# A mixture-of-experts stage: one region of rows per expert for all four batches, 39 blocks in an order made on the chip, results written back into their rows, first scatters spread over attention

## The chip, the core and the metric

The kernel runs on one core of one Trainium2 chip. The metric is the device time of one execution in microseconds (us).

## The reference, cut to what matters

The input is four batches of 1024 tokens of 128 features. Two transformer layers follow each other; the second is the one in question:

```python
x1 = layernorm(x + attention(x))              # 16 heads of 8, not causal
topk_p, topk_i = top_k(softmax(x1 @ Wg), 2)   # 8 experts, 2 per token
comb = one_hot(topk_i) * topk_p / sum(topk_p)
h = gelu(x1 @ W1[e] + b1[e])                  # 128 -> 512, for each expert e
y = h @ W2[e] + b2[e]                         # 512 -> 128
out = x + layernorm(x1 + sum_e comb[e] * y[e])
```

## The kernel before

Everything is written out by hand for each engine: TensorE, VectorE (DVE), ScalarE (ACT), GpSimd (POOL) and SyncE (SP), which issues nearly all plain DMAs in the order of its program. Semaphores join them.

**Attention.** The second layer's attention runs over 16 groups of four heads (0 to 15), four groups per batch. A group has 32 units; in each unit TensorE makes two score blocks (L613), ScalarE their exponentials (L709), TensorE the value products (L628), and for the next group a chunk of scores (L585) of which VectorE takes row maxima (L664). GpSimd stores each half of a group's head outputs (L750), prepares the next group's values and the maxima's bfloat16 parts (L758 on). Its `fronts` are called at point 0 (before the first store), 1 (before the maxima's parts) and 2 (after the second store).

**Fronts.** When a batch's four groups are done, its rows go through the output projection (L1467), the norm (roots on GpSimd, L1276), a transpose (L855), the gate's logits (L1480) and the choice of two experts. Batches 0 and 1 do so in groups 7 and 11, batch 2 in group 15, batch 3 beside the first blocks. `ranks` (L1484) counts on TensorE how many tokens chose each expert before this one; `sort` (L1771) turns that into a slot number for each token and choice.

**Scatter, blocks, gather.** `scatter` (L1299) writes each tile of 128 rows to its slots with an indirect DMA on GpSimd, two per tile. At most two are on the way: `ON_WAY`, `landed`. There are two sections: batches 0 and 1 (one sort in group 12), and batches 2 and 3 (two sorts). A section is worked off in 23 blocks of 256 rows, 2 x 16 x 128 / 256 = 16 full ones and up to 7 for the rests of 8 experts. `list_blocks` (L1795) works out on VectorE which expert a block belongs to. For block m, `load_expert` (L1080) fetches 578 KB of weights (4 buffers) and `load_rows` (L1089) 128 KB of rows (6 buffers); TensorE turns the rows (L1503), multiplies up (L1512), and multiplies down one block later (L1522). ScalarE makes the gelu (L2090), VectorE adds the bias (L1837), and `store_y` (L1104) writes the results to a second DRAM tensor. The experts and rows of the first blocks are loaded in group 14 (L1115 to L1130).

`gather` (L1315) picks each token's two results, eight indirect DMAs per half batch, two on the way in the first section and four in the second; VectorE combines them (L1840), GpSimd takes a root (L1334), ScalarE normalises (L2093), VectorE finishes (L1865), SP stores. The first section's gathers wait for its 23 blocks and run beside the second section; the second section's wait for all 46. The positions of all this in the block loop are written by hand (L904 to L909).

Numbers of a register are read by SP with `value_load`, for the expert of every block and, in the second section, for its rows.

## Time and profile before

| | us |
|---|---|
| median of three runs | 1621.58 |
| lowest, highest | 1619.73, 1623.44 |
| the profiled execution's own time | 1623.35 |
| its span in the trace | 1621.6 |

| engine | busy us | share |
|---|---|---|
| TensorE matmul | 1400.8 | 86% |
| VectorE | 1223.4 | 75% |
| ScalarE | 1141.0 | 70% |
| GpSimd | 481.0 | 30% |

The span is cut at attention's end (1363 us) and the last down (1559 us). Times in the rows count from the span's start. PE is TensorE, DVE VectorE, ACT ScalarE, POOL GpSimd, SPq SyncE's DMA queue. What stands in brackets behind a row is the engine's idle time before it and what ended that time.

### The profile page before, as it was taken

The page shows a single profiled execution, that of the slowest core. Times are in us where ns is not written, and L with a number is a line of the kernel's source. Part 1 is how long each engine was busy: PE and PEld are TensorE (multiplying, and loading weights), DVE is VectorE, ACT ScalarE, POOL GpSimd, SP SyncE. Part 2 cuts the span into 40 slices and gives each one's busy share as a digit, 9 for nine tenths or more (in the row PEclk, how much of TensorE's full clock was granted, in tenths as well). Part 3 has the DMA queues.
Part 4 walks back from the last instruction along what each step waited for, and adds up shares of the span by engine and source line. Part 5 has one row for each costly group of instructions (what it writes and reads, how often), then busy time and mean ns, then how long its engine had stood idle before and what let it go on. Part 6 is the DMA issues. An engine that isn't in the chain of part 4 may idle for free.

```text
span 1621.6 us, 36086 instructions
## 1 busy us (share of the span) xinstructions
PE 1400.8 (86%) x13425; PEld 604.9 (37%) x13425; DVE 1223.4 (75%) x1846; ACT 1141.0 (70%) x2357; POOL 481.0 (30%) x786
## 2 busy tenths in 40 slices
PE   5679999999998888479999999999988999899940
PEld 2323333333333555112222223222322235888830
DVE  6788888888881665799999998999898852432444
ACT  7628888888888455129999997999777786334421
POOL 5413333433334564200000003000314322332455
PEclk9959999999999999659999999999999899999975
DMA  4622212112112363401333331113101411778942
GB/s 137 196 79 74 69 41 72 55 56 74 44 51 75 100 178 95 152 5 48 118 126 125 106 89 43 42 49 90 36 28 62 133 38 59 217 232 242 275 134 57
DMA packets 130255, 158.26 MB, mean 98 GB/s; under 512 B 17312, under 2 KB 103328, under 8 KB 129824
## 3 DMA queue, kind: packets, MB, share of 16 engines
q1 hardware_dynamic: 120864, 130.77, 25.8%
q0 software_dynamic: 9216, 25.18, 4.5%
q8 instruction: 107, 1.75, 0.5%
q14 instruction: 68, 0.56, 0.1%
HBM read 90.90 MB, written 68.96 MB: 99 GB/s over the span
## 4 chain that ended last, share of the span: by engine, by line
PE 43%; DVE 10%; issue 6%; DMA 4%; ACT 2%; SPq 1%; POOL 1%; another core or an unknown queue 0%; POOLq 0%; DVEq 0%; ACTq 0%
PE bank L628 16%; PE banks L613 10%; DVE row_max L664 6%; PE banks L585 6%; PE banks L1522 4%; PE banks L1512 4%; DMA qk_parts<-parts 2%; ACT o_sums L724 1%; DMA parts<-sorted_in 1%; PE banks L1503 1%; PE banks L337 0%; PE banks L1467 0%; PE banks L1480 0%; DMA expert<-expert_rows 0%; DMA heads_out<-o_sums 0%
## 5 line engine op out<-in xcount | busy, mean ns | idle before, releaser
L664 DVE TENSOR_REDUCE row_max<-banks 128x2 f32<-128x1024 f32 (+3 forms) x896 | 936.4, 1104 | 77.5 <-PE banks L585 41.4
L709 ACT ACTIVATE probs<-banks 128x512 f32<-128x512 f32 (+3 forms) x1792 | 874.9, 552 | 134.8 <-PE banks L613 109.6
L628 PE MATMUL bank<-probs,v_ones 128*32 128x256 f32 (+2 forms) x6656 | 527.3, 389 | 11.7 <-ACT o_sums L724 10.5
L585 PE MATMUL banks<-k_work,q_work 48*128 48x512 bf16 (+3 forms) x1792 | 364.3, 379 | 62.9 <-DVE row_max L664 48.2
L613 PE MATMUL banks<-q_work,k_work 51*128 51x512 bf16 (+3 forms) x1792 | 383.8, 370 | 18.1 <-ACT probs L709 12.6
L613 PEld LDWEIGHTS banks<-q_work,k_work 51*128 51x128 bf16 x1792 | 105.6, 93 | 394.5 <-ACT probs L709 340.6
L628 PEld LDWEIGHTS bank<-probs,v_ones 128*32 128x32 f32 x6656 | 134.1, 108 | 262.5 <-ACT probs L709 169.5
L750 POOL DMA_DIRECT2D heads_out<-o_sums x64 | 36.7, 573 | 498.0 <-ACT o_sums L724 498.0
L2090 ACT ACTIVATE rope<-banks,expert 128x256 f32<-128x256 f32 x184 | 72.2, 475 | 111.6 <-PE banks L1512 96.9
L770 POOL TENSOR_SCALAR_AFFINE_SELECT probs<-probs 128x256 f32<-128x256 f32 x256 | 103.9, 409 | 124.8 <-ACT probs L709 124.1
L585 PEld LDWEIGHTS banks<-k_work,q_work 48*128 48x128 bf16 x1792 | 90.6, 96 | 120.0 <-DVE row_max L664 90.9
L1512 PE MATMUL banks<-rope,expert 128*128 128x256 f32 x368 | 89.6, 387 | 7.2 <-issue 6.6
L1522 PE MATMUL banks<-expert,rope 128*128 128x128 f32 x736 | 91.1, 278 | 0.8 <-DVE k_work L1837 0.8
L1522 PEld LDWEIGHTS banks<-expert,rope 128*128 128x128 f32 x736 | 87.1, 194 | 1.2 <-ACT rope L2090 0.8
L337 PE MATMUL banks<-hT,w_qk 128*128 128x512 f32 x128 | 67.2, 656 | 21.8 <-ACT hT L400 11.8
L1312 POOL DMA_INDIRECT sorted_in<-v_all,slots x64 | 62.0, 968 | 59.1 <-DMA sorted_in<-v_all,slots 45.3
L1512 PEld LDWEIGHTS banks<-rope,expert 128*128 128x128 f32 x368 | 67.7, 194 | 15.7 <-issue 8.1
L591 PE MATMUL banks<-later_keys,half_ident 64*128 64x128 bf16 (+1 forms) x1024 | 72.3, 210 | 0.0
L1829 DVE COPY rope<-banks 128x256 f32<-128x256 f32 x46 | 19.4, 422 | 64.4 <-PE banks L1503 53.9
L758 POOL CAST max_parts<-top_max 128x32 bf16<-128x32 f32 x32 | 6.7, 209 | 202.3 <-DVE top_max L672 202.3
L591 PEld LDWEIGHTS banks<-later_keys,half_ident 64*128 64x128 bf16 x1024 | 55.8, 99 | 23.4 <-issue 2.7
L383 POOL TENSOR_TENSOR parts<-probs,parts 128x1024 bf16<-128x1024 f32 x16 | 34.1, 2129 | 74.5 <-ACT parts L418 74.5
(195 smaller groups left out, 1035.0 us busy)
## 6 DMA issues: line engine op xcount, KB each, us to landing
expert<-expert_rows SPq DMA_DIRECT2D x46, 578.0 KB
qk_parts<-parts SPq DMA_DIRECT2D x64, 256.0 KB, 3.5
heads_out<-o_sums POOLq DMA_DIRECT2D x64, 256.0 KB, 4.2
sorted_in<-front SPq DMA_DIRECT2D x21, 512.0 KB, 6.1
q_work<-qk_parts SPq DMA_DIRECT2D x64, 128.0 KB
k_work<-qk_parts SPq DMA_DIRECT2D x64, 128.0 KB
parts<-sorted_in SPq DMA_DIRECT2D x46, 128.0 KB
q_work<-qk_parts SPq DMA_DIRECT2D x64, 64.0 KB
```

The costliest lines, as they stand in the source:

```text
L337: pe.matmul(bank[QK_BANK + u % QK_BANKS], w_qk[a][:, i, :], hT[:, :], start=True, stop=True).then_inc(s["qk"], 1)
L585: last = pe.matmul(to[:, par, 0:width], q[r:r + M0, pair, qt * P:(qt + 1) * P], k[r:r + M0, pair, kh * G:kh * G + width], start=True, stop ...
L591: last = pe.matmul(to[:, par, width - P + c0:width], half_ident[r:r + HALF, half, :], later_keys[r:r + HALF, half, c0:P], start=False, sto ...
L613: pe.matmul(to[par][:, 0:G - c0], k[r:r + M1, pair, kt * P:(kt + 1) * P], q[r:r + M1, pair, qh * G + c0:(qh + 1) * G], start=True, stop=Tr ...
L628: last = pe.matmul(bank[7][32 * j:32 * j + 32, c0 + c1:c0 + c1 + w], v_ones[i % QB][:, kt, j, :], prob_slots[:, (e + j) % RING, c1:c1 + w] ...
L664: dve.tensor_reduce(row_max[:, :, pair, qt, kh], self.buf_of("chunk", g, c)[:, :, 0:width], AX.X, ALU.max).then_inc(s["chunk_max"], 1)
L709: act.activation(prob_slots[:, e % RING, 0:width], self.ring_bank("exp", e)[:, 0:width], ACT.Exp, scale=SCALE).then_inc(s["exps"], 1)
L770: pool.affine_select(here, here, [[0, 2], [1, P]], ALU.is_ge, 0.0, base=0, channel_multiplier=-1).then_inc(s["blanked"], 1)
L1312: pool.indirect_dma_start(xs_d[section], bass.IndirectOffsetOnAxis(slots[:, section, i, tile:tile + 1], 0), x1_rows[:, ST * section + tile ...
L1512: last = pe.matmul(hidden(m, f), expert[:, m % W_BUFS, f * P:(f + 1) * P], xsT[:, m % 2, :], start=True, stop=True)
L1522: last = pe.matmul(bank[Y_BANK][:, side * P:(side + 1) * P], h_block[:, m % 2, f, side * P:(side + 1) * P], expert[:, m % W_BUFS, FF + f * ...
L2090: act.activation(h_block[:, m % 2, f, :], hidden(m, f), ACT.Gelu, bias=expert[:, m % W_BUFS, 2 * FF + f:2 * FF + f + 1]).then_inc(end["gel ...
```

## The change

There is one region of 4096 rows (16 blocks) for each expert in a single DRAM tensor, so that all four batches are worked off in 2 x 32 x 128 / 256 + 7 = 39 blocks. Each of the 128 possible blocks of the regions is a candidate, one per partition. `list_grades` gives each a grade: blocks filled by batches 0 and 1 first, then those filled with batch 2, then the others. TensorE spreads the keys to all partitions, VectorE counts the lower ones, and the result is the list of block rows and experts. FULL is (9, 17, 25): so many blocks are surely full after batch 1, 2 and 3. The list is made in two parts, for blocks 0 to 16 after batch 2's sort and for 17 to 38 at blocks 11 to 13 of the loop. Rows of block 9 wait for batch 2's scatters, those of block 17 for batch 3's. DONE is (25, 31, 39): after 25 stored blocks batches 0 and 1 are complete, after 31 batch 2, after 39 batch 3. `store_y` writes to the rows that the block was read from; the gathers use the scatters' own slots, with four on the way (GATHERED). The scatters of the first section are issued one tile at a time, each behind a wait for ScalarE's exponentials of a given unit, in groups 12 to 15. The loads of the first experts and rows go from group 14 to behind the sums of batch 3. The tensor to be zeroed has 32 runs of 512 KB in place of 23. `place` and the old list go.

```diff
-BLOCKS = TOPK * ST // SIDES + E - 1
...
+BLOCKS = TOPK * B * TILES // SIDES + E - 1
...
+SEEN = (ST, ST + TILES, ST + 2 * TILES)
+FULL = tuple(-(-(TOPK * n * P - E * (BR - 1)) // BR) for n in SEEN)
+HELD = tuple((TOPK * n * P + E * (BR - 1)) // BR for n in SEEN)
+LISTED = (0, FULL[1], BLOCKS)
+LISTS = len(LISTED) - 1
+READY = (0, FULL[0], FULL[1])
+DONE = (max(FULL[1] + E, HELD[0]), HELD[1], BLOCKS)
...
-        SCATTER_AT = ((0, 1, 0, 3), (0, 2, 3, 10), (1, 1, 10, 12), (1, 2, 12, ST))
+        SCATTER_AT = ((0, 1, 20),) + tuple((g, at, u) for g in (1, 2) for at, u in ((0, 3), (0, 7), (0, 11), (0, 15), (1, 20)))
+        SCATTER_AT += ((3, 0, 11), (3, 0, 14), (3, 0, 17), (3, 1, 20), (3, 1, 23))
...
-        ROWS_FROM, ROWS_LATE = BLOCKS - 3, (2, 2, 1)
-        LOAD_AT, COMBINE_AT, MOMENTS_LATE = (4, 8, 12, 16, 18, 21), (8, 13, 17, 22), (9, 14, 18)
-        NORMAL_AT, FINISH_AT, OUT_AT = (13, 18, 22), (14, 19), (15, 20)
-        ROWS_FROM, ROWS_LATE = BLOCKS - 3, (2, 2, 1)
+        LIST_AT = (11, 12, 13)
+        AHEAD_OF = {FULL[0]: 2, FULL[1]: 2}
+        LOAD_AT, COMBINE_AT, MOMENTS_LATE = (20, 21, 22, 23), (31, 34, 37), (32, 35, 38)
+        NORMAL_AT, FINISH_AT, OUT_AT = (34, 37), (35, 38), (37,)
         FOLD_UNIT, PRODUCT_FIRST, APPLY_FIRST, TURN_FIRST, INPUT_FIRST = 2, 8, 14, 17, 19
...
             def load_expert(m):
-                section, j = divmod(m, BLOCKS)
-                sp.wait_ge(end["blocks"], section + 1)
+                sp.wait_ge(end["blocks"], 1 if m < LISTED[1] else 2)
                 if m >= W_BUFS:
                     sp.wait_ge(end["y"], m - W_BUFS + 1)
-                which = sp.value_load(block_expert[0:1, section, j:j + 1], min_val=0, max_val=E - 1)
+                which = sp.value_load(block_expert[0:1, m:m + 1], min_val=0, max_val=E - 1)
                 sp.dma_start(expert[:, m % W_BUFS, :], expert_d[bass.ds(which, 1), :, :].rearrange("o p r -> (o p) r")
                              ).then_inc(w_here[m % W_BUFS], 16)
 
             def load_rows(m):
-                section, j = divmod(m, BLOCKS)
-                if j == 0:
-                    wait_lanes(sp, scatter_number(section * (STAGES - 1), TOPK * (TILES if section else ST) - 1))
+                if m in READY:
+                    stage = READY.index(m)
+                    wait_lanes(sp, scatter_number(stage, TOPK * (ST if stage == 0 else TILES) - 1))
+                sp.wait_ge(end["blocks"], 1 if m < LISTED[1] else 2)
                 if m >= X_BUFS:
-                if section:
-                    sp.wait_ge(end["blocks"], section + 1)
-                    which = sp.value_load(block_row[0:1, j:j + 1], min_val=0, max_val=REGION - 1)
-                    src = rows[bass.ds(which, 1), :, :, :].rearrange("o p k d -> (o p) k d")
-                else:
-                    src = rows[j, :, :, :]
+                which = sp.value_load(block_row[0:1, m:m + 1], min_val=0, max_val=REGION - 1)
+                src = xs_blocks[bass.ds(which, 1), :, :, :].rearrange("o p k d -> (o p) k d")
                 sp.dma_start(xs_in[:, m % X_BUFS, :, :], src).then_inc(xs_here[m % X_BUFS], 16)
 
             def store_y(m):
-                section, j = divmod(m, BLOCKS)
                 sp.wait_ge(end["y"], m + 1)
-                to = ys_d[section].rearrange("(n k p) d -> n p k d", k=SIDES, p=P)[j, :, :, :]
-                sp.dma_start(to, y_of(m)).then_inc(y_out[section], 16)
+                which = sp.value_load(block_row[0:1, m:m + 1], min_val=0, max_val=REGION - 1)
+                to = xs_blocks[bass.ds(which, 1), :, :, :].rearrange("o p k d -> (o p) k d")
+                sp.dma_start(to, y_of(m)).then_inc(y_out[done_of(m)], 16)
 
...
-                if i == NG - 2:
-                    sp.wait_ge(mid["x_out"], 16 * GROUPS)
-                    sp.wait_ge(rows_made, 16 * len(made))
-                    for m in range(W_BUFS):
-                        load_expert(m)
 
...
             attend[2].load_sums(sp, B - 1)
+            sp.wait_ge(mid["x_out"], 16 * GROUPS)
+            sp.wait_ge(rows_made, 16 * len(made))
+            for m in range(2):
+                load_expert(m)
+                load_rows(m)
             attend[2].store_reciprocals(sp, B - 1)
-            load_expert(W_BUFS)
+            for m in range(2, W_BUFS):
+                load_expert(m)
+                load_rows(m)
             for k in range(HALVES):
                 load_front(B - 1, k)
...
+            loaded_rows = W_BUFS
+            for m in range(BLOCKS):
+                if 0 < m and m + W_BUFS - 1 < BLOCKS:
+                    load_expert(m + W_BUFS - 1)
+                while loaded_rows < min(m + X_BUFS, BLOCKS):
+                    late_from = max((x for x in AHEAD_OF if x <= loaded_rows), default=None)
+                    if late_from is not None and m < late_from - AHEAD_OF[late_from] + (loaded_rows - late_from) // 2:
+                        break
+                    load_rows(loaded_rows)
+                    loaded_rows += 1
...
             def gather(n):
                 section, h = divmod(n, SETS)
-                if h == 0:
-                    pool.wait_ge(y_out[section], 16 * BLOCKS)
-                    if section:
-                        pool.wait_ge(end["placed"], 1)
+                if n % HALVES == 0 and n != HALVES:
+                    pool.wait_ge(y_out[max(n // HALVES - 1, 0)], 16 * (DONE[0], DONE[1] - DONE[0], DONE[2] - DONE[1])[max(n // HALVES - 1, 0)])
                 if section:
                     pool.wait_ge(end["sum"], GT * (n - SETS + 1))
...
-                for group, at, a, b in SCATTER_AT:
+                for tile, (group, at, u) in enumerate(SCATTER_AT):
                     if (i, point) == (SORT_GROUP + group, at):
-                        scatter(0, a, b)
+                        pool.wait_ge(attend[2].s["exps"], i * attend[2].ne + 2 * u)
+                        scatter(0, tile, tile + 1)
...
+            def list_keys(n, to):
+                pe.wait_ge(end["keyed"], 2 * n + 1)
+                pe.matmul(to[:, 0:P], ones_b[:, :], graded[:, :], start=True, stop=True).then_inc(end["listed"], 1)
+
+            def list_rows(n, to):
+                a, b = LISTED[n:n + 2]
+                pe.wait_ge(end["keyed"], 2 * n + 2)
+                pe.matmul(to[:, P:P + b - a], ids_b[:, :], found[:, 0:b - a], start=True, stop=True)
+                pe.matmul(to[:, 2 * P:2 * P + b - a], experts_b[:, :], found[:, 0:b - a], start=True,
+                          stop=True).then_inc(end["listed"], 1)
+
...
             pe.wait_ge(attend[2].s["exps"], NG * attend[2].ne)
+            list_keys(0, bank[LIST_BANK[0]])
+            list_rows(0, bank[LIST_BANK[0]])
             turn_rows(0)
...
+            def count(stage):
+                a, b = STAGE_TILES[stage]
+                n = b - a
+                dve.wait_ge(end["ranks"], stage + 1)
+                base = seen[:, stage - 1:stage, :] if stage else region[:, :, :]
+                total = rank_bank(stage)[:, n * E:(n + 1) * E].rearrange("p (o e) -> p o e", o=1)
+                link(dve.tensor_tensor(seen[:, stage:stage + 1, :], total, base, ALU.add))
...
-                    list_blocks(0)
-                    link(dve.tensor_scalar(first_slot[:, :, :], start_of[:, :, :], float(SIDES * P), None, ALU.mult))
-                link(dve.tensor_tensor(slot_te[:, a:b, :], within, base[:, :, :].broadcast_to([P, n, E]), ALU.add))
+                link(dve.tensor_tensor(slot_te[:, a:b, :], within, base.broadcast_to([P, n, E]), ALU.add))
                 for i in range(TOPK):
                     last = dve.tensor_tensor(slot_pick[:, i, a:b, :], chosen[:, i, a:b, :], slot_te[:, a:b, :], ALU.mult)
...
-            def list_blocks(section):
...
-            def place():
...
+            def list_grades(n):
+                stages = n + 2
+                link(dve.tensor_tensor(seen_own[:, 0:stages, :], seen[:, 0:stages, :],
+                                       own_expert[:, :, :].broadcast_to([P, stages, E]), ALU.mult))
+                link(dve.tensor_reduce(filled[:, 0:stages], seen_own[:, 0:stages, :], AX.X, ALU.add))
+                link(dve.tensor_scalar(filled[:, 0:stages], filled[:, 0:stages], own_start[:, 0:1], None, ALU.subtract))
+                dve.tensor_scalar(whole[:, 0:stages], filled[:, 0:stages], float(BR), None, ALU.is_ge)
+                link(dve.tensor_scalar(begun[:, 0:stages], filled[:, 0:stages], 1.0, None, ALU.is_ge))
+                nearer, among = (whole[:, 0:1], whole[:, 1:2]) if n == 0 else (begun[:, 1:2], begun[:, 2:3])
+                link(dve.tensor_tensor(grade[:, :], begun[:, 0:1], nearer, ALU.add))
+                link(dve.scalar_tensor_tensor(grade[:, :], grade[:, :], 1.0, among, ALU.add, ALU.mult))
+                if n:
+                    link(dve.scalar_tensor_tensor(grade[:, :], taken[:, :], 0.0, grade[:, :], ALU.is_equal, ALU.mult))
+                    link(dve.tensor_tensor(grade[:, :], grade[:, :], taken[:, :], ALU.subtract))
+                link(dve.tensor_scalar(grade[:, :], grade[:, :], -1.0, 3.0, ALU.mult, ALU.add))
+                dve.tensor_tensor(own_key[:, :], own_share[:, :], grade[:, :], ALU.add)
+                dve.tensor_scalar(graded[:, :], ident_b[:, :], grade[:, 0:1], None, ALU.mult).then_inc(end["keyed"], 1)
+
+            def list_places(n, to):
+                a, b = LISTED[n:n + 2]
+                dve.wait_ge(end["listed"], 2 * n + 1)
+                link(dve.tensor_tensor(keys[:, :], to[:, 0:P], row_share[:, :], ALU.add))
+                link(dve.tensor_scalar(lower[:, :], keys[:, :], own_key[:, 0:1], None, ALU.is_lt))
+                link(dve.tensor_reduce(place[:, :], lower[:, :], AX.X, ALU.add))
+                if n == 0:
+                    dve.tensor_scalar(taken[:, :], place[:, :], float(b), None, ALU.is_lt)
+                dve.tensor_scalar(found[:, 0:b - a], row_ids[:, 0:b - a], place[:, 0:1], None, ALU.is_equal).then_inc(end["keyed"], 1)
+
+            def list_blocks(n, to):
+                a, b = LISTED[n:n + 2]
+                dve.wait_ge(end["listed"], 2 * n + 2)
+                dve.tensor_copy(block_row[:, a:b], to[:, P:P + b - a])
+                dve.tensor_copy(block_expert[:, a:b], to[:, 2 * P:2 * P + b - a]).then_inc(end["blocks"], 1)
 
```

## Rows read from the trace of the kernel before

**Rows 1.** The page's 40 slices of 40.5 us, TensorE's busy tenths.

```profile
PE   5679999999998888479999999999988999899940
```

**Rows 2.** Busy time per stretch (us), granted clock, DMA share, GB/s.

```profile
1470.00:1480.00 10.00, 10.00 (x70) 9.33 (x70) 2.12 (x5) 3.96 (x11) 1.96 (x2) 1.00 0.80 240
```

**Rows 3.** TensorE's timeline (start, us, engine, line), ups of two blocks.

```profile
1471.06 1.89 PE L1512 MATMUL banks<-rope,expert 128*128 128x256 f32 x8
...
1474.79 1.89 PE L1512 MATMUL banks<-rope,expert 128*128 128x256 f32 x8
```

**Rows 4.** GpSimd's timeline, gathers, first and last of each bunch.

```profile
1477.64 1.00 POOL L1331 DMA_INDIRECT probs<-sorted_out,slots  x1 [23.18 <-DMA sorted_out<-q_work]
...
1512.11 0.95 POOL L1331 DMA_INDIRECT probs<-sorted_out,slots  x1 [1.97 <-DMA probs<-sorted_out,slots]
...
1563.33 1.02 POOL L1331 DMA_INDIRECT probs<-sorted_out,places  x1 [0.58 <-issue]
...
1604.58 0.94 POOL L1331 DMA_INDIRECT probs<-sorted_out,places  x1 [0.30 <-issue]
```

**Rows 5.** GpSimd's timeline, stores of head outputs, two per group of heads.

```profile
1107.34 0.56 POOL L750 DMA_DIRECT2D heads_out<-o_sums  x1 [11.35 <-ACT o_sums L724]
...
1125.73 0.54 POOL L750 DMA_DIRECT2D heads_out<-o_sums  x1 [17.42 <-ACT o_sums L724]
...
1144.58 0.56 POOL L750 DMA_DIRECT2D heads_out<-o_sums  x1 [11.39 <-ACT o_sums L724]
...
1217.05 0.61 POOL L750 DMA_DIRECT2D heads_out<-o_sums  x1 [19.91 <-ACT o_sums L724]
...
1238.31 0.63 POOL L750 DMA_DIRECT2D heads_out<-o_sums  x1 [10.78 <-ACT o_sums L724]
...
1266.54 0.59 POOL L750 DMA_DIRECT2D heads_out<-o_sums  x1 [4.77 <-ACT o_sums L724]
...
1287.12 0.61 POOL L750 DMA_DIRECT2D heads_out<-o_sums  x1 [11.35 <-ACT o_sums L724]
...
1307.88 0.59 POOL L750 DMA_DIRECT2D heads_out<-o_sums  x1 [3.40 <-ACT o_sums L724]
```

**Rows 6.** VectorE's timeline, first sort: first step and the slots' step.

```profile
1199.54 0.16 DVE L1780 COPY total_of<-banks 128x8 f32<-128x8 f32 x1
...
1202.06 0.29 DVE L1783 TENSOR_TENSOR slot_te<-banks,first_slot 128x128 f32<-128x128 f32 x1
```

**Rows 7.** TensorE's timeline within group 13.

```profile
1256.35 0.59 PE L613 MATMUL banks<-q_work,k_work 51*128 51x512 bf16 x1 [2.15 <-issue]
```

**Rows 8.** TensorE's timeline, ups of blocks 0 and 5.

```profile
1363.90 1.96 PE L1512 MATMUL banks<-rope,expert 128*128 128x256 f32 x8 [0.61 <-DVE rope L1829]
...
1387.63 2.83 PE L1512 MATMUL banks<-rope,expert 128*128 128x256 f32 x8
```

**Rows 9.** SyncE's DMA issues: the sums, then block 24's expert, rows, store.

```profile
1367.70 0.60 SPq L508 DMA_DIRECT2D sums_in<-heads_out  x1
...
1472.67 0.35 SPq L1086 DMA_DIRECT2D expert<-expert_rows  x1
1473.85 0.38 SPq L1102 DMA_DIRECT2D parts<-sorted_in  x1
1474.27 0.47 SPq L1108 DMA_DIRECT2D sorted_out<-q_work  x1
```

**Rows 10.** GpSimd's timeline: last store, a root, scatters of batches 2 and 3.

```profile
1363.88 0.54 POOL L750 DMA_DIRECT2D heads_out<-o_sums  x1 [16.62 <-ACT o_sums L724]
...
1398.94 1.01 POOL L1276 TENSOR_TENSOR rstd<-ve,minus_half 128x4 f32<-128x4 f32 x1 [1.85 <-DVE minus_mean L1678]
...
1406.54 0.96 POOL L1312 DMA_INDIRECT sorted_in<-v_all,slots  x1 [0.30 <-issue]
...
1419.37 1.03 POOL L1312 DMA_INDIRECT sorted_in<-v_all,slots  x1 [1.29 <-DVE slots L1793]
...
1453.51 0.96 POOL L1312 DMA_INDIRECT sorted_in<-v_all,slots  x1 [1.61 <-DMA sorted_in<-v_all,slots]
```

344 lines of the change are left out of this document (156 added, 188 removed).

## The prediction

> **What bounds the kernel now.** The page's slices come first [rows 1]: TensorE is busy in eight or nine tenths of nearly every slice up to the last two, where it stands still. So there are three stages to read: attention (to 1363 us), the expert blocks (to 1559 us) and a tail without TensorE (to 1621.6 us).
>
> The stretches of ten microseconds show the block stage more finely [rows 2]: 10.00 of 10 us of TensorE at full clock (1.00, the 2.4 GHz level), DMA share 0.80 before any gather runs. The TensorE timeline gives the price of a block [rows 3]: up to up, 1474.79 - 1471.06 = 3.73 us. Blocks set the pace there, and DMA has little room left.
>
> In the tail the chain is GpSimd's gathers: eight per half batch, 32 of them from 1563.33 to 1604.58, one after the other, then 16.1 us from the end of the last (1605.5) to the span's end [rows 4].
>
> In attention the group of four heads has a steady beat: between two stores of the head outputs 18.39 and 18.85 us, 37.2 us per group [rows 5]. The groups in which the first two batches' rows are scattered are longer.
>
> **Attention, what goes.** (a) The first sort loses its block list: VectorE from the copy at 1199.54 to the sort's own first step at 1202.06 is 2.5 us [rows 6], in a stretch where VectorE's maxima pace the group. Added there is one 8-column addition of 0.2 us. Gain 2.3 us. (b) The scatters. Excess of the half groups over the steady halves [rows 5]: group 12 second half 21.26 - 18.85 = 2.4, group 13 first half 28.23 - 18.39 = 9.8, second half 20.58 - 18.85 = 1.7, group 14 first half 20.76 - 18.39 = 2.4; 16.3 us together, worst where the timeline has 14 scatters between two stores (GpSimd then still waits 4.77 us for ScalarE, so the store is not late by itself). There TensorE idles 2.15 us with nothing to wait for [rows 7]: a freeze behind the bunch. The change issues two scatters at a time, four units (about 4.7 us) apart. Bounds: it saves nothing and adds 3 us (ten scatters now lie in group 15), or it saves all 16. I take 11, two thirds, because the bunches of four to eight cost 2 us and the bunch of fourteen 9.8. The other new waits of GpSimd hold up its stores and maxima parts: those have their input at units 18 and 23, the waits end at 17 and 20 (23 once), so only a microsecond of slack is used: nothing. The 32 fills instead of 23 (16.8 MB instead of 12) run in groups 1 to 4 beside TensorE's work; if that cover were gone, nine more at the 240 GB/s of the block stage [rows 2] would cost 2.2 us each, 20 us. The iotas and the candidates' nine small VectorE steps lie in group 0 and 15, where those engines wait anyway. Attention: -13.3 us.
>
> **The start of the blocks.** Before, four experts and five row blocks are loaded in group 14 and the first up starts at 1363.90. After, the block list needs batch 2, so SP may load experts only behind the sums. VectorE's grades are done in attention's last units; TensorE's two small steps and VectorE's four end near 1365.4. SP however is busy till 1367.70 + 0.6 with the sums. A value read costs SP 0.8 us: from the end of the expert issue at 1473.02 to the row issue at 1473.85 [rows 9]. First expert issued 1369.1, its rows 1370.3; landing estimated at 3.9 us from the last store of 256 KB, issued 1363.88 and awaited till 1367.70 [rows 9, 10]. First up near 1374, ten microseconds late. But before, blocks 0 to 4 took 23.7 us for five times 3.73, because a row load stood behind the sums and the heads [rows 8]; after, those loads come before they are due, and the up of block 5 starts near 1393.5 instead of 1387.63: +5.9 us (bounds +3 and +9).
>
> **Two new waits of SP.** Block 9's rows are only fetched once all 16 scatters of batch 2 have landed. The last four stand behind the two roots of batch 3 (VectorE's moments of blocks 5 and 6): root at 1398.94, fourth issue at 1406.54 [rows 10], so last landing near 1410, with the shift 1416; SP reads and issues, 2.5 us for the rows: 1419. They are due after the up of block 8, 1409.2 with the shift. Stall 10 us plus 1 for the clock (bounds 4 and 14). Queued behind SP's wait are one store and one expert load, both early enough. Before, this had 14 blocks of room.
>
> Block 17's rows need all of batch 3. Its slots come 6.5 us after the up of block 10, 1436 by now. The 16 scatters took 1419.37 to 1453.51 [rows 10], 2.28 us each with two on the way. Block 17's rows are due only at 1454.5, when nine are issued; then SP blocks, its loads dry up, and the remaining seven go at 2.3 falling to 1.3 us. Last landing 1468, rows there 1471.5: stall 17 us, up of block 17 at 1474.7 with slow matmuls. Bounds 8 and 22. The spread grades and keys replace a long list on VectorE there; with TensorE stalled twice anyway I count no gain, and the new keys' matmuls, each shorter than a row's transposes, cost nothing beside it.
>
> **End of the blocks.** Up of block 25: 1474.7 + 8 x 3.73 + 1.0 = 1505.6. Up of block 38: 13 x 3.73 later, 1554.1; the last down ends near 1560.5, against 1559.1 before. So the seven blocks that go (7 x 3.73 = 26.1 us) are spent on the start and the two stalls.
>
> **The gathers.** Before, 32 start at 1477.64 beside the blocks and 32 more at 1563.33. After, all 64 form one chain from the 25th block's store. Its down lies between the ups of blocks 25 and 26, so its result is there at 1509.5; SP then has three value reads per block (expert, rows, store: 3 x 0.8 + 1.2 = 3.6 us against the block's 3.73, no room to catch up), 3.2 us, plus 2 us of backlog from the two rows per block after the stall and the four loads of x; from store to first gather 3.4 us (1474.27 to 1477.64) [rows 4, 9]. First gather 1518.1. Two roots (2 us each) and the rest of 39 us pass while experts still load, at c us per gather: 35/c gathers. The others take 1.25 us, with three roots between them. G = 39 + (64 - 35/c) x 1.25 + 6 = 125 - 44/c. The row has c = 2.3 with two on the way (16 from 1477.64 to 1512.11) and the issue itself allows 1.25 (32 and a root in 41.25 us) [rows 4]; four on the way is new. I take c = 1.5, G = 96 (bounds 90 and 106), nearer to the issue because the share of 0.80 leaves some room.
> The page DMA: Bandwidth & Descriptors of the Trainium skill, section on queues, rings and completion order, says that each DMA engine takes turns between the queues it has work for, packet by packet. By that rule GpSimd's queue would get its turn however full SP's is; it is weighed below as a rival, and no row here has four gathers beside the loads.
>
> **The sum.** 1518.1 + 96 + 16.1 - 13.3 = 1616.9 against the span of 1621.6: -4.8 with rounding. The profiled execution's own time was 1623.35, the median of the three runs 1621.58; I put the difference on the median: 1616.8 us. What a measurement of this kernel can tell from no change is about 0.2%, 3.2 us.
>
> **Rivals.**
> *Gathers held back (slower).* Four on the way only lengthen each landing, since the loads fill most of the DMA engines. c stays 2.3, G 106: 1626.6. For it: the share of 0.80 before they begin [rows 2]. Against: gathers are 64 KB each. It ends slower from c = 2.1 up. Chance 0.15.
> *Gathers keep the issue's pace.* Landings of 4.6 us (two times 2.3) with four on the way would hide under four issues of 1.25: c = 1.25, G 90, 1611. Chance 0.10. The Trainium skill's turn-taking between queues, above, would make this the case.
> *The pacing saves nothing.* The freezes belong to each scatter, not to the bunch: +11, 1627.8. Against: 9.8 us in one half only. Chance 0.12.
> *The waits are short.* With fewer row loads the scatters land faster, stalls of 4 and 8 us: -15, near 1602. For it: rows 9 and on are not fetched meanwhile, 128 of 850 KB per block. Against: two on the way, as before [rows 10]. Chance 0.16.
> *SP becomes the bound.* A fourth part more per value read gives 4.2 us per block: from block 17 to 25 +4, 1621, no change. Chance 0.09.
> *The change does not pace or order anything in time* (GpSimd comes late to each named unit; the list is free): as before apart from the tail, no change. Chance 0.04.
> Forecast as summed: 0.34, its own range 1609 to 1625: 0.24 of it below 1618.3, 0.07 within, 0.03 above 1624.8.
>
> **Numbers.** Faster by over 0.2%: 0.16 + 0.10 + 0.24 = 0.50. Within: 0.09 + 0.04 + 0.07 = 0.20. Slower: 0.15 + 0.12 + 0.03 = 0.30. The range reaches from the short waits to the held gathers together with part of the lost pacing: 1601 to 1635.
>
> **What would show it.** The half groups 12 to 14 near 19 to 20 us each, no idle of 2 us with nothing waited for. First up 10 us after attention's end. TensorE idle 10 us before the rows of block 9 and 17 us before block 17, with the granted clock lower behind each. 39 ups, the last near 1541 in the new span. First gather near 1505, with c between 1.25 and 1.8 while experts load, then 1.25; the gathers without a pause from set to set. I am wrong if the stall at block 17 is under 8 us, if the start costs over 15 us, or if the tail after the last down is not within 10 us of the 62.5 of before: that would mean the gather chain was not what ends last.

## The result, and the profile after

| | before | after |
|---|---|---|
| median of 20 runs each, us | 1619.83 | 1611.22 |
| lowest to highest, us | 1611.61 to 1626.31 | 1606.11 to 1618.04 |
| the profiled execution's own time, us | 1623.35 | 1607.74 |
| its span, us | 1621.6 | 1605.8 |

The ratio is 0.9956, its 95% interval 0.9942 to 0.9970: a gain of 0.44%, some 7 us. The two profiled executions are 15.8 us apart, twice as much, because single executions of one kernel lie up to 15 us apart. So the profiles serve to find stages, and the medians to say what a stage is worth.

GpSimd's timeline of the kernel after, stores of the head outputs around groups 12 to 14 (start, us, engine, line, operation; in brackets the idle time before and what ended it):

```profile
1213.61 0.61 POOL L761 DMA_DIRECT2D heads_out<-o_sums  x1 [16.94 <-ACT o_sums L735]
...
1232.45 0.63 POOL L761 DMA_DIRECT2D heads_out<-o_sums  x1 [11.39 <-ACT o_sums L735]
...
1250.85 0.58 POOL L761 DMA_DIRECT2D heads_out<-o_sums  x1 [2.56 <-ACT o_sums L735]
...
1270.46 0.61 POOL L761 DMA_DIRECT2D heads_out<-o_sums  x1 [11.35 <-ACT o_sums L735]
...
1288.85 0.58 POOL L761 DMA_DIRECT2D heads_out<-o_sums  x1 [2.57 <-ACT o_sums L735]
```

They answer to [rows 5]. Group 12's second half takes 18.8 us instead of 21.3, group 13's halves 18.4 and 19.6 instead of 28.2 and 20.6, group 14's first 18.4 instead of 20.8. From the store ahead of group 12 to the last store it is 152.2 us instead of 172.8.

TensorE's timeline of the kernel after: the first rows and ups, then blocks 9, 17 and 25, the last up and the last down:

```profile
1351.93 0.69 PE L1509 MATMUL banks<-ident,parts 128*128 128x128 f32 x2 [8.32 <-DMA parts<-sorted_rows]
1353.22 3.75 PE L1518 MATMUL banks<-rope,expert 128*128 128x256 f32 x8 [0.61 <-DVE rope L1858]
...
1375.45 1.89 PE L1518 MATMUL banks<-rope,expert 128*128 128x256 f32 x8
...
1398.54 0.69 PE L1509 MATMUL banks<-ident,parts 128*128 128x128 f32 x2 [8.21 <-DMA parts<-sorted_rows]
1399.02 3.62 PE L1528 MATMUL banks<-expert,rope 128*128 128x128 f32 x16
...
1448.24 0.69 PE L1509 MATMUL banks<-ident,parts 128*128 128x128 f32 x2 [14.40 <-DMA parts<-sorted_rows]
...
1452.14 2.78 PE L1518 MATMUL banks<-rope,expert 128*128 128x256 f32 x8
...
1484.16 1.99 PE L1518 MATMUL banks<-rope,expert 128*128 128x256 f32 x8 [0.40 <-DMA expert<-expert_rows]
...
1534.16 1.89 PE L1518 MATMUL banks<-rope,expert 128*128 128x256 f32 x8
...
1539.09 2.02 PE L1528 MATMUL banks<-expert,rope 128*128 128x128 f32 x16 [1.25 <-DVE k_work L1865]
```

Three long waits for rows are new: 8.32, 8.21 and 14.40 us (before, the two that there were took 3.62 us, at block 5, and 1.41), each followed by matmuls at half speed (the 16 of a down in 3.62 us instead of 1.95). The 39 blocks need as long from attention's end (1341.83) to the last down's end (1541.1) as the 46 did: 199.3 us, before 196.

GpSimd's gathers in the kernel after, the 1st, 16th, 32nd, 33rd and 64th:

```profile
1496.86 0.99 POOL L1333 DMA_INDIRECT probs<-sorted_rows,slots  x1 [53.04 <-DMA sorted_rows<-v_ones]
...
1516.65 0.95 POOL L1333 DMA_INDIRECT probs<-sorted_rows,slots  x1 [0.30 <-issue]
...
1541.91 0.94 POOL L1333 DMA_INDIRECT probs<-sorted_rows,slots  x1 [0.30 <-issue]
...
1544.74 1.01 POOL L1333 DMA_INDIRECT probs<-sorted_rows,slots  x1 [0.54 <-issue]
...
1588.62 0.95 POOL L1333 DMA_INDIRECT probs<-sorted_rows,slots  x1 [0.30 <-issue]
```

They answer to [rows 4] and form one chain: 92.7 us from the first to the end of the last (1589.57), then 16.2 us to the span's end. While experts still load a gather comes every 1.32 us (15 steps in 19.79 us), before every 2.3 us.

The page's slices of the kernel after, busy tenths in 40.1 us each, answering to [rows 1], and one stretch beside the blocks (the columns of [rows 2], to which it answers):

```profile
PE   5679999999998888469999999999999997779930
...
DVE  6788888888892465699999999999999952231345
...
POOL 5413333334333565300000002100222333240575
```

```profile
1500.00:1510.00 10.00, 10.00 (x70) 9.23 (x69) 2.12 (x5) 3.50 (x10) 6.99 (x8) 1.00 0.91 290
```

TensorE has nothing in the last slice and little in the one before, where VectorE and GpSimd are busy with what follows the gathers. Beside the gathers TensorE is still full at the upper clock level (1.00, 2.4 GHz), with the DMA engines at 0.91 instead of 0.80.

### The profile page after: what moved, and what is told of

It is laid out like the page before. It is cut to its first block, busy times and chain, and to the rows that moved or that the text cites. A ratio compares the mean times of both kernels' runs of the same rounds, so it can differ in the third digit from the quotient of the medians.

```text
span 1605.8 us, 35919 instructions
## 1 busy us (share of the span) xinstructions
PE 1368.5 (85%) x13249; PEld 585.1 (36%) x13249; DVE 1215.3 (76%) x1842; ACT 1130.6 (70%) x2329; POOL 481.9 (30%) x789
## 4 chain that ended last, share of the span: by engine, by line
PE 34%; DVE 10%; DMA 7%; issue 6%; POOL 5%; SPq 3%; ACT 2%; POOLq 0%; ACTq 0%; DVEq 0%
PE bank L639 15%; PE banks L624 9%; DVE row_max L675 7%; PE banks L596 5%; POOL probs L1333 3%; DMA sorted_rows<-v_all,slots 2%; DMA qk_parts<-parts 2%; PE banks L1528 1%; DMA probs<-sorted_rows,slots 1%; PE banks L1518 1%; ACT o_sums L735 1%; DMA parts<-sorted_rows 1%; DMA sums_in<-heads_out 1%; SPq L1133 1%; PE banks L348 1%
## 5 line engine op out<-in xcount | busy, mean ns | idle before, releaser
L596 PE MATMUL banks<-k_work,q_work 48*128 48x512 bf16 (+3 forms) x1792 | 359.5, 377 | 61.7 <-DVE row_max L675 49.0
L624 PE MATMUL banks<-q_work,k_work 51*128 51x512 bf16 (+3 forms) x1792 | 376.9, 368 | 10.9 <-ACT probs L720 9.9
L2127 ACT ACTIVATE rope<-banks,expert 128x256 f32<-128x256 f32 x156 | 61.2, 475 | 115.4 <-PE banks L1518 115.4
L1333 POOL DMA_INDIRECT probs<-sorted_rows,slots x64 | 62.8, 982 | 76.1 <-DMA sorted_rows<-v_ones 53.0
L1518 PE MATMUL banks<-rope,expert 128*128 128x256 f32 x312 | 79.2, 399 | 2.9 <-DMA expert<-expert_rows 1.7
L1317 POOL DMA_INDIRECT sorted_rows<-v_all,slots x64 | 62.5, 977 | 62.6 <-DMA sorted_rows<-v_all,slots 30.1
L1528 PE MATMUL banks<-expert,rope 128*128 128x128 f32 x624 | 79.5, 283 | 1.3 <-DVE k_work L1865 1.3
L1858 DVE COPY rope<-banks 128x256 f32<-128x256 f32 x39 | 16.5, 423 | 82.0 <-PE banks L1509 82.0
L1528 PEld LDWEIGHTS banks<-expert,rope 128*128 128x128 f32 x624 | 76.2, 199 | 1.5 <-issue 1.4
L1518 PEld LDWEIGHTS banks<-rope,expert 128*128 128x128 f32 x312 | 59.1, 200 | 11.5 <-DMA expert<-expert_rows 2.4
```

What stands on the lines that cost most here:

```text
L596: last = pe.matmul(to[:, par, 0:width], q[r:r + M0, pair, qt * P:(qt + 1) * P], k[r:r + M0, pair, kh * G:kh * G + width], start=True, stop ...
L624: pe.matmul(to[par][:, 0:G - c0], k[r:r + M1, pair, kt * P:(kt + 1) * P], q[r:r + M1, pair, qh * G + c0:(qh + 1) * G], start=True, stop=Tr ...
L1317: pool.indirect_dma_start(xs_d, bass.IndirectOffsetOnAxis(slots[:, section, i, tile:tile + 1], 0), x1_rows[:, ST * section + tile, :], Non ...
L1333: pool.indirect_dma_start(y_picked[:, h, i, g, :], None, xs_d, bass.IndirectOffsetOnAxis(slots[:, section, i, tile:tile + 1], 0)).then_inc ...
L1518: last = pe.matmul(hidden(m, f), expert[:, m % W_BUFS, f * P:(f + 1) * P], xsT[:, m % 2, :], start=True, stop=True)
L1528: last = pe.matmul(bank[Y_BANK][:, side * P:(side + 1) * P], h_block[:, m % 2, f, side * P:(side + 1) * P], expert[:, m % W_BUFS, FF + f * ...
```

## The experiments

Each median is of 7 to 12 runs beside 14 to 31 runs of the kernel before on the same chip. There were four chips, A to D.

| run | chip | median us | before us | ratio, interval |
|---|---|---|---|---|
| e0, after unchanged | A | 1610.99 | 1620.62 | 0.9958 [0.9936, 0.9981] |
| e1, after, scatters bunched | A | 1618.98 | 1620.62 | 0.9994 [0.9974, 1.0014] |
| e2, before, scatters paced | A | 1609.48 | 1620.62 | 0.9928 [0.9901, 0.9956] |
| e3, after, tiles first | B | 1633.03 | 1631.07 | 1.0014 [0.9991, 1.0037] |
| e4, after, four on the way | B | 1641.17 | 1631.07 | 1.0066 [1.0043, 1.0089] |
| e5, after, two gathers | B | 1630.35 | 1631.07 | 1.0005 [0.9983, 1.0027] |
| e6, e3 and e4 together | B | 1642.85 | 1631.07 | 1.0073 [1.0050, 1.0096] |
| f0, after unchanged | C | 1634.01 | 1632.15 | 1.0015 [0.9993, 1.0038] |
| f1, as e2 | C | 1617.33 | 1632.15 | 0.9906 [0.9870, 0.9941] |
| f2, after, four then wait | C | 1631.10 | 1632.15 | 0.9996 [0.9968, 1.0024] |
| f3, after, loads ahead | C | 1644.52 | 1632.15 | 1.0088 [1.0059, 1.0117] |
| g1, e2 and a later sum | D | 1607.52 | 1620.17 | 0.9929 [0.9904, 0.9954] |

**What each half of the change is worth.** e0 is the kernel after once more.

> The changed kernel once more, on the chip and in the rounds of the next two. Theory A (the pair of profiles is typical): 0.990 of before, since the profiles differ by 15.8 us. Theory B (the profile of before showed longer freezes than most executions, or that of the change shorter ones): 0.9956 as in the 20 runs, 7 us, and the profile's groups 12 to 15 again take about 152 us (in the first profile 41.9, 38.0, 37.8 and 34.6).

e1 takes the pacing back:

```diff
-        SCATTER_AT = ((0, 1, 20),) + tuple((g, at, u) for g in (1, 2) for at, u in ((0, 3), (0, 7), (0, 11), (0, 15), (1, 20)))
-        SCATTER_AT += ((3, 0, 11), (3, 0, 14), (3, 0, 17), (3, 1, 20), (3, 1, 23))
+        SCATTER_AT = ((0, 1, 0, 3), (0, 2, 3, 10), (1, 1, 10, 12), (1, 2, 12, ST))
...
-                        pool.wait_ge(attend[2].s["exps"], i * attend[2].ne + 2 * u)
-                        scatter(0, tile, tile + 1)
+                        scatter(0, a, b)
```

> The change, but with the scatters of the first two batches in the bunches of before. Theory A: groups 12 to 15 grow by 15 to 18 us as in the profile of before and the time is 1.0 us above or below before's, ratio about 1.000. Theory B: the freeze behind a bunch is there in only some executions; groups grow by 3 to 8 us and the ratio is 0.997 to 1.000. Rival (pacing was worth nothing, the list on VectorE was all): groups as in the changed kernel, ratio equal to that of the run before this one.

e2 (and f1) is the reverse: the same lines of pacing put into the kernel before, nothing else.

> The kernel before, with nothing changed but that its first scatters are paced as in the change; the first row blocks are loaded some 30 us later for that, but still before attention ends. Theory A: groups 12 to 15 shrink by 15 us and the time by as much, ratio 0.990. Theory B: ratio 0.995 to 0.998. If the regions and the 39 blocks are what brings the gain, the ratio is 1.000. Group 12's first half keeps its 26 us, since the long list on VectorE stays (23.0 in the changed kernel).

> The kernel before with only the pacing of the first scatters, a second time. Theory: the pacing is worth all of the change, 9 to 12 us: ratio 0.990 to 0.995 on any chip, within 0.3% of the kernel after where the gathers run undisturbed, and faster than it by more where they are disturbed, since here half of the gathers stand before the last blocks with room behind them. Rival, the first reading was luck of one chip: ratio 0.997 to 1.000.

Measured: e1 lies 8.0 us above e0, e2 11.1 us under the kernel before, f1 14.8 us under it on chip C. So the pacing is worth 8 to 15 us wherever it is put. The rest of the change (regions, 39 blocks, the order made on the chip) is worth the difference between after and e2: on chip A the medians are 1.5 us apart, the ratios 0.003 with 0.0036 uncertainty, so no gain; on chip C the kernel after is 16.7 us slower than f1. All of the measured gain is the pacing's.

What a bunch costs shows in two ways. First the kernel before, TensorE's and VectorE's timelines while the 14 scatters of group 13 are issued:

```profile
1252.71 0.60 PE L585 MATMUL banks<-k_work,q_work 48*128 48x512 bf16 x2
...
1256.39 1.23 DVE L664 TENSOR_REDUCE row_max<-banks 128x2 f32<-128x1024 f32 x1 [3.03 <-remote]
...
1261.38 1.23 DVE L664 TENSOR_REDUCE row_max<-banks 128x2 f32<-128x1024 f32 x1 [3.77 <-remote]
```

"Remote" says that the profile names no instruction and no transfer of this core as what ended the wait. The semaphore behind it is nevertheless one that TensorE raises: the chunk of scores whose maxima VectorE takes at 1256.39 ended at 1253.31 (first line), and the trace records the semaphore's rise at 1256.36. The same step lies 4.0 us apart at the second row. With TensorE's idle of [rows 7] this is what the prediction called a freeze. In e1 the same bunch gives no such row; there GpSimd itself is late and TensorE waits for it (TensorE's timeline of e1):

```profile
1275.53 0.26 PE L610 MATMUL banks<-ident_b,max_parts 128*96 128x128 bf16 x1 [3.27 <-POOL max_parts L775]
```

In e1 the half with the bunch took 23.9 us, in e0 18.4. Over the four halves from group 12's second to group 14's first the trace of before has 90.8 us, that of e1 81.1, those of after, e0 and e2 75.2: the profiled execution of before shows 15.6 us of bunches, that of e1 5.8, with medians of 11.1 and 8.0 between them. From 1215 to 1290 us the paced kernels (after, e0, e2) have no wait of either kind over 1 us.

**Which wait of the block stage is on the path.** e3 scatters the last two tiles of batch 2 ahead of the two roots:

```diff
-            scatter(1, 0, TILES - 2)
+            scatter(1, 0, TILES)
             for k in range(HALVES):
                 end_root(B - 1, k)
-            scatter(1, TILES - 2, TILES)
```

> The kernel after with the second stage's last two tiles scattered ahead of the two tail set-up steps, so that the whole of the first stage's rows is in place sooner. Theory: the stall in front of block 9 (8.2 to 15.5 us step) is a wait for those last scatters, and the chain blocks -> 25th store -> 64 gathers passes through it; then the step into block 9 falls from about 15 us to 5 us or less, but the wait in front of block 17 stays where the second stage's scatters end, so it grows by part of that. Expected: first gather up to 3 us earlier, total 1608 to 1611 (0 to -3 us against the kernel after). Rival, the end hangs on the second stage's scatters alone: step into 9 gone, step into 17 grows by the same, total unchanged within 1 us. Rival, the stall in front of block 9 is another transfer's: step into 9 stays at 15.

The step into block 9 fell from 15.5 (e0; 16.0 in e5 on the same chip, not changed up to there) to 11.6 us, the one into block 17 stayed at 19.6, and from the last store to the first gather it is 149.6 us against 154.4 in e0, 153.8 in e5 and 153.9 in f0. So 4 us of the wait are those scatters'. The total did not show it: on chip B the time after the first gather grew (below).

f3 loads the first four experts and row blocks right after the last maxima's loads, ahead of the sums:

```diff
+                if i == NG - 2:
+                    sp.wait_ge(mid["x_out"], 16 * GROUPS)
+                    sp.wait_ge(rows_made, 16 * len(made))
+                    for m in range(W_BUFS):
+                        load_expert(m)
+                        load_rows(m)
...
-            for m in range(2):
...
             attend[2].store_reciprocals(sp, B - 1)
-            for m in range(2, W_BUFS):
...
```

> The kernel after with the first four experts and the first four blocks' rows loaded one group earlier, while attention still runs, as the kernel before does. Theory (GpSimd's chain sets the end: second and third stage's scatters, block 17, the 25th store, 64 gathers; the 10 us in front of the first block are not on it): first up within 1 us of the last head store instead of 10.4 after it, the step into block 9 grows by 7 to 10 us to 22 to 25, the step into block 17 and the first gather stay, total within 2 us of the kernel after. Rival, the start is on the path: everything behind comes 8 to 10 us sooner, total 1601 to 1603 where the kernel after has 1611.

Both theories missed: 10.5 us slower than f0. SyncE's queue in f3:

```profile
1357.03 0.38 SPq L1101 DMA_DIRECT2D expert<-expert_rows  x1
1358.37 0.39 SPq L1113 DMA_DIRECT2D parts<-sorted_rows  x1
...
1365.64 0.38 SPq L1113 DMA_DIRECT2D parts<-sorted_rows  x1
1366.13 0.62 SPq L519 DMA_DIRECT2D sums_in<-heads_out  x1
```

The loads could not leave sooner: TensorE's two matmuls that make the list run at 1355.3, behind attention's last values, with the last store at 1354.6. So SyncE stood at the first load (the rival, that the start is on the path, was not put to the test by this edit), and the sums left 11.5 us after the last store (f0: 1352.38 - 1350.0 = 2.4). VectorE holds the reciprocal of these sums ahead of the first block's copy:

```profile
1370.24 0.95 DVE L530 RECIPROCAL sums_rcp<-sums_in 128x128 f32<-128x128 f32 x1 [14.48 <-DMA sums_in<-heads_out]
1371.11 0.36 DVE L1856 COPY rope<-banks 128x256 f32<-128x256 f32 x1
```

First up 17.0 us after the last store instead of 10.6, the first gather 161.0 instead of 153.9; the steps into blocks 9 and 17 stay within 1 us (15.3 and 19.6, f0: 15.2 and 20.6), since the scatters behind batch 3's front moved with it. That is the chain: sums, front of batch 3, scatters of batches 2 and 3, block 17, the 25th store, 64 gathers. It passes through SyncE's and VectorE's queues. The sums' delay of 9.1 us came out as 7.1 at the first gather and, counted from the last store, as 7.0 at the span's end (287.6 us, f0: 280.6). The other 3.5 of the 10.5 us between the medians are not traced: the last store itself is 4.6 us later in this trace, about as much as between the two traces of the kernel after (4.4).

**More scatters on their way.**

```diff
-ON_WAY = (2, 2, 2)
+ON_WAY = (2, LANES, LANES)
```

> The kernel after with four instead of two scatters allowed on their way in the two later stages. Theory: the 14 to 16 us in front of block 17 are GpSimd waiting for the landing of the scatter two back (a scatter's round trip, about 3.6 us for two), so with four the second stage's scatters go at their issue pace of 1.3 us or so and end some 8 to 10 us sooner; the step into 17 falls from 20 to about 11 us, the first gather comes 8 us sooner, total 1602 to 1604 (-8 us against the kernel after). Rival, the scatters are held by their landing rate whatever the number on the way: step into 17 stays at 19 to 20, total 1611. Rival, the scatters finish sooner but the end goes by GpSimd's own work: first gather 8 us sooner and total within 2 us of 1611.

> The kernel after with both edits: the second stage's last two tiles ahead of the set-up of the tail, and four scatters on their way in the two later stages. Theory (the chain scatters of stages 1 and 2 -> blocks 9 and 17 -> 25th store -> gathers sets the end): steps into 9 and 17 fall to 5 and 10 to 14 us, first gather 10 to 14 us sooner, total 1598 to 1602. Rival, the blocks are freed but the last transfer chain (32nd gather to last block) is bound elsewhere: first gather sooner by 10, total only 0 to 4 us less than 1611.

Missed, in a way that tells most. The step into block 17 did fall, from 19.6 to 10.1 us, but a step of 16.1 us appeared at block 14. The last three of the 16 scatters in e4, then TensorE's turned rows for block 14 with VectorE's copy of them, and TensorE's up:

```profile
1442.38 0.96 POOL L1317 DMA_INDIRECT sorted_rows<-v_all,slots  x1 [0.30 <-issue]
1443.65 0.96 POOL L1317 DMA_INDIRECT sorted_rows<-v_all,slots  x1 [0.30 <-issue]
1444.91 0.96 POOL L1317 DMA_INDIRECT sorted_rows<-v_all,slots  x1 [0.30 <-issue]
```

```profile
1431.99 0.38 PE L1509 MATMUL banks<-ident,parts 128*128 128x128 f32 x2
...
1445.77 0.42 DVE L1858 COPY rope<-banks 128x256 f32<-128x256 f32 x1 [9.50 <-remote]
```

```profile
1446.29 2.05 PE L1518 MATMUL banks<-rope,expert 128*128 128x256 f32 x4 [10.29 <-issue]
```

GpSimd issues 16 scatters in an unbroken row from 1425.35; VectorE and TensorE stop in the middle of it and go on as the last has been issued (1445.87). The blocks' inputs were there: TensorE waits for VectorE's copy, and VectorE for TensorE's rows, which had been turned by 1432.37; the semaphore that says so rose at 1445.69. e4 is 8.1 us slower than e3 on the same chip, e6 9.8 (steps of 11.1 and 11.6 us at blocks 14 and 15).

**Gathers beside the blocks.**

```diff
-GATHERED = (LANES, LANES)
+GATHERED = (2, LANES)
```

> The kernel after with the gathers of the first two batches held to two on their way, as in the kernel before, instead of four. If the second of the change's small edits is worth what I put on it, these 32 gathers go at 1.6 to 2.3 us each instead of 1.4: the stretch from first to 33rd gather grows from 48 to 53 to 70 us and the total by the same minus nothing, as the last 32 gathers can't start before: 1617 to 1630. Rival, the expert loads don't slow a gather and a gather lands in under twice its issue time: cadence stays 1.3, total within 2 us of 1611.

> The kernel after, unchanged, beside the kernel before on one more chip. On one chip the ratio was 0.996 with no stop of TensorE over 5 us while the gathers ran. On another, kernels that differ from after by one line had three to four stops of 4 to 16 us while GpSimd issued gathers without a pause, and 1630 to 1633 us. If the stops belong to the chip: here either none and 1608 to 1614 us with the kernel before near 1620, or three to four and near 1632 with the kernel before near 1631. Rival, the stops belong to the moved lines: none here on any chip, ratio 0.994 to 0.997.

On chips B and C the kernel after has no gain: 1.0015 in f0, and e3, one line from it, 1.0014. Up to the first gather f0 and e0 differ by 2.3 us (1503.88 and 1501.54), to the 33rd by 21.4 (1569.6 and 1548.2), and from there to the last both take 43.8. f0 within that stretch, a down on TensorE, gathers on GpSimd, then VectorE, ScalarE and TensorE:

```profile
1508.90 1.95 PE L1528 MATMUL banks<-expert,rope 128*128 128x128 f32 x16
...
1511.86 0.94 POOL L1333 DMA_INDIRECT probs<-sorted_rows,slots  x1 [0.72 <-DMA probs<-sorted_rows,slots]
...
1523.10 0.94 POOL L1333 DMA_INDIRECT probs<-sorted_rows,slots  x1 [0.30 <-issue]
1526.60 0.42 DVE L1865 TENSOR_TENSOR v_ones<-banks,expert 128x256 f32<-128x256 f32 x1 [10.86 <-remote]
1526.69 1.57 ACT L2127 ACTIVATE rope<-banks,expert 128x256 f32<-128x256 f32 x4 [12.65 <-remote]
...
1527.17 3.75 PE L1528 MATMUL banks<-expert,rope 128*128 128x128 f32 x16 [7.59 <-ACT rope L2127]
```

and its stretches, busy time of each engine, granted clock, DMA share, GB/s:

```profile
1504.00:1514.00 10.00, 6.86 (x50) 6.23 (x48) 0.85 (x2) 3.09 (x8) 7.45 (x8) 1.00 0.82 265
1514.00:1526.00 12.00, 3.74 (x10) 2.84 (x10) 0.42 (x1) 0.04 (x1) 7.61 (x9) 0.71 0.24 68
```

A row of ten gathers runs 1.25 us apart. Meanwhile TensorE does one up (at 1515.84) and VectorE one copy, ScalarE nothing for 12.65 us, and the DMA engines are at 0.24, so bandwidth is not what is short. Neither is a fetch of instructions: the profile's two instruction queues moved no packet between 1504 and 1531 us. Runtime: NRT & Kernel Launch of the Trainium skill, section on instruction fetch mechanics, has each engine fetch its code through a DMA queue of its own in blocks of 16 KiB; that stays out as the cause by this count.

What is late can be told. What VectorE starts at 1526.60 waits for the down of the first line alone, which TensorE ended at 1510.86; TensorE has since made an up and turned the next rows (to 1519.58). The trace records when the semaphores rose that tell of these three pieces of work: 1526.58, 1526.67 and 1526.71, all within 0.13 us of each other. So the work was done and the news of it was held back, by up to 15.7 us. It is the same at each of the waits of VectorE and ScalarE over 4 us that the traces of e3, e4, e6, f0, f1 and f3 put down to "remote" from 1100 us on: the semaphore is one that TensorE raises, 1.9 to 15.9 us after the work that it tells of.

The stop also costs GpSimd: its 17th gather stands behind a root that needs VectorE's sum, which is placed behind block 31, so it comes at 1542.1, 19.0 us after the 16th (e0: 2.9).

In e5 the first 16 gathers come 2.0 us apart instead of 1.3, and the 32 together take 61.7 us to the 33rd, between e0's 46.7 and f0's 65.8. Its trace has no wait over 2 us put down to "remote": with a pause for a landing between most gathers no stop appears, on a chip where e3 has 16 us steps. The longest waits that it has beside them (5.6 us on TensorE, 9.8 on ScalarE) stand behind a sum on VectorE that waits 6.1 us for gathered rows. So the slower gathers cost about what the stops did.

f2 lets four go and then waits for all of them:

```diff
-                        landed(at - GATHERED[section])
+                        landed(at - (1 if section == 0 and at % LANES == 0 else GATHERED[section]))
```

> The kernel after, where each fourth gather of the first two batches waits until all issued before it have landed (seven pauses of some 1 to 2 us). On a chip without stops: the 32 gathers take 8 to 14 us more, total +8 to +14 us against the kernel after. On a chip with stops, theory that an unbroken row of gathers holds the other engines up: the stops over 4 us are gone, TensorE's blocks 25 to 38 take 3.8 us each, total within 3 us of the kernel after or below it. Rival, any gathers under way stop the others: stops as before, total 8 to 14 us above.

```profile
1511.16 0.94 POOL L1333 DMA_INDIRECT probs<-sorted_rows,slots  x1 [0.30 <-issue]
1514.38 0.94 POOL L1333 DMA_INDIRECT probs<-sorted_rows,slots  x1 [2.28 <-DMA probs<-sorted_rows,slots]
```

With these pauses TensorE, VectorE and ScalarE have no wait over 4 us put down to "remote" or "issue" from 1100 us to the end (f0: eight), TensorE's longest step behind block 18 is 6.3 us (f0: 14.9), and the last up comes 13.6 us sooner although the first came 3.4 us later. The total is 2.9 us under f0, within the uncertainty, since the pauses themselves cost the chain what the stops did. That an unbroken row brings the stops is shown on this chip, and by e4 and e5 on chip B; that TensorE's semaphores are what comes late is shown too, but not what holds them back. Why chips B and C have them beside gathers and chip A does not is open, and so is whether the 10 to 12 us that the kernel before itself needs more on B and C are of the same kind: no trace of it was taken there. The paced one (f1) has two such stops on chip C, 6.0 and 5.5 us, beside a row of eight scatters at attention's end, where g1 on chip D has a row as long and no stop.

**The kernel before, paced, with a later sum.** In e2 and f1 VectorE waits 5.5 and 7.1 us for the gathers of its third sum, with a block's copy queued behind (VectorE's timeline of f1):

```profile
1526.18 1.14 DVE L1854 SCALAR_TENSOR_TENSOR probs<-probs,pw,v_all 128x128 f32<-128x128 f32 x4 [7.09 <-DMA probs<-sorted_out,slots]
```

```diff
-        ..., COMBINE_AT, MOMENTS_LATE = ..., (8, 13, 17, 22), (9, 14, 18)
+        ..., COMBINE_AT, MOMENTS_LATE = ..., (8, 13, 20, 22), (9, 14, 21)
```

> The kernel before with the pacing of the first scatters, and with VectorE's third sum of gathered rows put behind the second section's block 20 instead of block 17 (its statistics behind block 21 instead of 18). In the kernel before with pacing alone VectorE stood 5.5 and 7.1 us in front of that sum (row of the scaled addition, released by the gather's landing), with the copies of the next blocks' rows queued behind it, and TensorE's step into up 42 was 8.9 and 10.5 us. Theory: the end of this kernel still goes by TensorE's blocks, so the step falls to about 4 us, the last up and the 33rd gather come 5 to 7 us sooner: ratio to the kernel before 0.985 to 0.990, that is 4 to 6 us under pacing alone. Rival, the wait moves to block 20 or the 33rd gather waits for the fourth sum: ratio as with pacing alone, 0.990 to 0.993.

The step into up 42 (8.9 and 10.5 us) is gone and the last up comes 182.5 us after the first instead of 187.5 (e2). But the 33rd gather now comes 9.15 us after the last down's start instead of 6.3: the fourth sum waits 2.88 us for its gathers and a root stands between. The ratio is that of e2, 0.993. So the fastest form measured is the kernel before with the pacing alone (e2, f1); it beats the kernel after by 16.7 us on chip C and is level with it on A.

## Why the prediction was right

1616.8 us was forecast and 1611.2 measured, "faster" held. By its steps:

- **Attention, -13.3.** The list's 2.3: group 12's first half 26.0 became 23.0. The pacing's 11 (a choice of two thirds of 16.3): 15.6 in the profiled pair, 8.0 and 11.1 between medians on chip A, 14.8 on C. Right in size. The reason given, a freeze, covers one of the two ways: e1 loses time through GpSimd's late maxima. And [rows 7] is no idle with nothing to wait for: that matmul waits for ScalarE's exponentials, which began at 1255.69 behind an idle of 2.56 us of their own. Attention ended 21.1 us sooner in the profiled pair, where 13.3 were forecast.
- **Start, up of block 5 +5.9.** From attention's end to that up 33.6 us instead of 24.7: +8.9, at the upper bound. The first up came 11.4 us after attention's end, 10 were forecast; the wait for the rows (8.32 us) was foreseen, the two ups at half speed behind it (3.75 us each) were not.
- **The two new waits, 10 and 17 us.** 8.21 and 14.40, for the reason given, the scatters of batches 2 and 3; e3 and e4 each shortened the step that they were aimed at. With the matmuls at half speed behind them the steps are 11.3 and 16.5 us longer than 3.73. The scatters of batch 3 ran from 1415.69 to 1442.86, 1.8 us each and not 2.28.
- **Seven blocks given back.** The last down ended at 1541.1; with attention's 21.1 us put back that is 1562.2, and 1560.5 was forecast.
- **First gather 1518.1.** 1496.86 plus the same 21.1 is 1518.0.
- **Length of the gather chain G, the mis-sized term.** 96 was taken, 92.7 came (91.4 in e0), since c was 1.3 and not 1.5. That is nearly the rival "gathers keep the issue's pace" (c 1.25), which was given a chance of 0.10 and priced at 1611. By that rule, turn-taking between queues (DMA: Bandwidth & Descriptors of the Trainium skill, section on queues, rings and completion order), c is 1.25, and these two traces agree: with the DMA engines at 0.91 (the stretch above) a gather still came every 1.3 us.

So 3.3 of the 5.6 us by which the forecast was too high are G's. Another 1.8 are the base: 1621.58 was the median of three runs of the kernel before, 1619.83 is that of twenty. The rest is within what executions of one kernel differ by. By parts the forecast was -13.3 for attention and +8.6 for everything behind it. On chip A the pacing alone brings 8.0 to 11.1 us, and the rest of the change costs 1.5, or some 4 without the list's 2.3: a smaller gain less a smaller cost. That the sign came out as forecast also depended on the chip, and that was luck: on B and C the same change brings nothing.

The tail behind the last down is 64.7 us long, within 10 us of 62.5, so that sign of being wrong did not show. "Gathers held back" was right on chips B and C in its time (G 110.5 in f0, from 1503.88 to the last one's end at 1614.3; 106 and 1626.6, slower, were priced, and the measured ratio there is 1.0015, no change) and wrong in its mechanism: the gathers kept their pace in each row, and it was the other engines that were held up. "The pacing saves nothing" and "the waits are short" fell with e2 and with the 14.40 us. "SP becomes the bound" priced 4.2 us per block from 17 to 25, the forecast 3.73; it was 4.0 (1452.14 to 1484.16), but block 17 had come 1.5 us sooner than forecast (1473.2 with the 21.1, 1474.7), so that the first gather was on time. A small misreading: [rows 1] has TensorE busy in 4 tenths of the last slice but one, so it stands still in the last alone.

## What to carry to other kernels

Issue indirect DMAs a few at a time, with a pause between, wherever other engines have work and the DMAs themselves are not what ends last: pacing 32 scatters was worth 0.5 to 0.9%, in both kernels on chip A and in the kernel before on chip C, and allowing more of them on their way made the kernel slower. Where a chain of them sets the end, as these gathers do, pauses took away the stops and gave no time clear of the noise (e5, f2). Fewer units in the stage that fills the profile give nothing by themselves if the last queue in line (here 64 gathers behind the 25th store) starts no sooner: price the start and each new wait first. Time a gain of half a per cent on more than one chip before you believe it.

## What was not expected of the hardware

- An unbroken row of indirect DMAs on GpSimd, 1.25 us apart, can hold up TensorE, VectorE and ScalarE for 4 to 16 us, with the DMA engines at 0.24 of their time and no instruction packet moved. What comes late is the rise of semaphores that TensorE raises, up to 15.9 us after the work that they tell of, and several then rise within 0.13 us. The stop ends about when the row ends (e4: the last issue is over at 1445.87, VectorE goes on at 1445.77; f0: 1524.04 and 1526.60). Pauses of 2 to 4 us after each four (f2), or two on their way instead of four (e5), prevent the long ones.
- Beside gathers it depended on the chip. The three traces of the kernel after and e1 on chip A and the result's chip have no such wait over 4 us; the five with four gathers on their way and no added pause on chips B and C (e3, e4, e6, f0, f3) all have some. Between e0 and f0 the stretch from the first to the 33rd gather is 19.1 us longer by it, of 23.0 between the medians, and the kernel before is slower on chip C too, by 11.5. So the gain is gone there.
